# First routing stage: at most two of GpSimd's indexed scatters under way

## What is computed

```python
scores = jax.nn.sigmoid(x @ gate_w.T)                       # 32 experts
_, topk_ids = jax.lax.top_k(scores + e_bias[None, :], 4)
topk_w = jnp.take_along_axis(scores, topk_ids, axis=1)
topk_w = topk_w / jnp.sum(topk_w, axis=1, keepdims=True)
combine = zeros((T, E)).at[arange(T)[:, None], topk_ids].add(topk_w)
a = silu(einsum('th,ehi->tei', x, w1)) * einsum('th,ehi->tei', x, w3) * combine[:, :, None]
out = einsum('tei,eih->th', a, w2)
```

## Time and profile before

| | us |
|---|---|
| runs of the kernel before | 1258.39, 1265.16, 1267.11 (median 1265.16) |
| the profiled execution | 1277.19 |
| its span, first to last instruction | 1275.4 |
| first scatter issued | 329.91 |
| last scatter issued | 538.32 |
| first load of a list issued | 555.88 |
| first TensorE instruction of the experts' stage | 559.33 |

### The profile page before, as it was taken

How to read it: one execution, slowest core, us unless ns; L and a number is a source line. 1 busy time by engine, 2 the same in 40 slices (tenths; PEclk the granted TensorE clock), 3 DMA queues, 4 the chain that set the end, 5 groups by cost and what they waited for, 6 DMA issues and landing times. The chain is left out here.

```text
span 1275.4 us, 27327 instructions
## 1 busy us (share of the span) xinstructions
PE 941.0 (74%) x10334; PEld 714.0 (56%) x10334; DVE 717.1 (56%) x1742; ACT 572.5 (45%) x960; POOL 613.5 (48%) x582
## 2 busy tenths in 40 slices
PE   1478778875576655449995139888898889995998
PEld 1356566654232222149995017777777777885565
DVE  3455555542567555625554256566676776654565
ACT  1156666664566455326664013333333333332554
POOL 1256767564567746614444772453544631111454
PEclk9997888785778777769998578899899998998999
DMA  5221111101746945677775610413224223000001
GB/s 143 68 71 61 51 53 53 53 2 55 266 180 232 293 162 194 239 214 201 202 202 166 252 42 20 155 54 121 86 89 155 82 89 114 22 2 1 10 26 34
DMA packets 112065, 144.04 MB, mean 113 GB/s; under 512 B 14325, under 2 KB 93090, under 8 KB 105794
## 3 DMA queue, kind: packets, MB, share of 16 engines
q1 hardware_dynamic: 73026, 110.68, 25.6%
q0 software_dynamic: 8192, 16.79, 4.3%
q10 hardware_dynamic: 30720, 14.82, 4.0%
HBM read 76.60 MB, written 65.40 MB: 111 GB/s over the span
## 5 line engine op out<-in xcount | busy, mean ns | idle before, releaser
L917 POOL DMA_INDIRECT fetched_a<-rows_y,chosen_row x128 | 122.6, 958 | 172.9 <-DVE att_a L810 120.9
L438 POOL TENSOR_TENSOR p_lo_a<-probs_a,p_hi_a 128x1024 f16<-128x1024 f32 x64 | 136.3, 2129 | 88.3 <-ACT p_hi_a L297 88.1
L1474 POOL DMA_INDIRECT rows_x<-rows_r,index_r x128 | 136.1, 1063 | 79.4 <-DVE index_r L1378 42.5
L617 PEld LDWEIGHTS psum<-v_x_a,probs_a 128*128 128x128 f32 x1024 | 127.9, 201 | 3.4 <-issue 0.3
L617 PE MATMUL psum<-v_x_a,probs_a 128*128 128x65 f32 x1024 | 128.8, 282 | 0.0
L1652 POOL TENSOR_TENSOR h_lo_t<-hidden_t,h_hi_t 96x512 f16<-96x512 f32 x48 | 55.4, 1154 | 94.2 <-ACT h_hi_t L1620 94.2
L354 DVE TENSOR_REDUCE negmax_a<-psum 128x8 f32<-128x1024 f32 x64 | 78.2, 1223 | 23.4 <-PE psum L168 23.0
L795 DVE TENSOR_REDUCE negmax_a<-psum 128x8 f32<-128x1024 f32 x64 | 78.2, 1222 | 20.1 <-PE psum L602 9.7
L296 ACT ACTIVATE probs_a<-psum 128x1024 f32<-128x1024 f32 x64 | 65.5, 1023 | 45.4 <-PE psum L152 45.4
L668 PE MATMUL psum<-wo,att_t_a 128*128 128x128 f32 x512 | 63.9, 278 | 8.2 <-ACT att_t_a L729 5.8
L1398 DVE TENSOR_TENSOR k_out_r<-psum,k_out_r 128x512 f16<-128x512 f32 x64 | 42.1, 686 | 48.7 <-issue 29.3
(11 more groups left out here) (336 smaller groups left out, 2989.3 us busy)
## 6 DMA issues: line engine op xcount, KB each, us to landing
values<-v_out_r SPq DMA_DIRECT2D x16, 1040.0 KB
v_x_a<-values SPq DMA_DIRECT2D x16, 1040.0 KB
keys<-k_out_r SPq DMA_DIRECT2D x16, 1024.0 KB
listed_t<-rows_x SPq DMA_DIRECT2D x96, 128.0 KB, 2.3
rows_y<-result_t ACTq DMA_DIRECT2D x48, 256.0 KB, 2.4
k_a_a<-keys SPq DMA_DIRECT2D x16, 512.0 KB
k_b_a<-keys SPq DMA_DIRECT2D x16, 512.0 KB
q_pad_a<-narrow_q SPq DMA_DIRECT2D x64, 64.0 KB
```

What stands on the lines that cost most here:

```text
L438: nc.gpsimd.tensor_tensor(p_lo[:, s % RING0, :], probs[:, s % NPR, :], p_hi[:, s % RING0, :], ALU.subtract).then_inc(s_plo, 1)
L617: last_ = nc.tensor.matmul(PV[:, part, i * (HD + 1):(i + 1) * (HD + 1)], probs[:, s % 3, lane(part, i)], v_x[:, par, b % GB, h, :], start= ...
L917: nc.gpsimd.indirect_dma_start(fetched[:, b % NF1, k, :], None, rows_y, bass.IndirectOffsetOnAxis(ap=chosen["row"][:, b, k:k + 1], axis=0) ...
L1474: nc.gpsimd.indirect_dma_start(rows_x, bass.IndirectOffsetOnAxis(ap=index[:, g * GB + t, k:k + 1], axis=0), rows[:, g % 2, t, :, :].rearra ...
```

## The change

Scatter n of the stage, counted over all groups, first waits until scatter n - 2 has landed. For that the semaphore is chosen by the parity of n instead of that of the group. The wait on ScalarE is rewritten for the new counting: both semaphores must show that all scatters of groups up to g - 2 have landed. The final wait on SP (`s_scatter[0]` and `s_scatter[1]` at 256 x 4 each) stays as it is, 64 scatters of 16 on each.

```diff
@@ upper_rows(g), ScalarE @@
                     act.wait_ge(s_xhat, g + 1)
                     if g >= 2:
-                        act.wait_ge(s_scatter[g % 2], 256 * (g // 2))
+                        for n in range(2):
+                            act.wait_ge(s_scatter[n], 8 * 16 * (g - 1))
                         act.wait_ge(s_turn, g - 1)
@@ GpSimd @@
                     for t in range(GB):
                         for k in range(K0):
+                            n = (g * GB + t) * K0 + k
+                            if n >= 2:
+                                pool.wait_ge(s_scatter[n % 2], 16 * (n // 2))
                             nc.gpsimd.indirect_dma_start(
                                 rows_x, bass.IndirectOffsetOnAxis(ap=index[:, g * GB + t, k:k + 1], axis=0),
-                                rows[:, g % 2, t, :, :].rearrange("p h d -> p (h d)"), None).then_inc(s_scatter[g % 2], 16)
+                                rows[:, g % 2, t, :, :].rearrange("p h d -> p (h d)"), None).then_inc(s_scatter[n % 2], 16)
```

## The result

| | before | after |
|---|---|---|
| runs, us | 1258.39 to 1276.07, 4 runs, median 1266.13 | 1291.20 to 1298.85, 4 runs, median 1294.51 |
| ratio, 95% interval | 1 | 1.0234 [1.0195, 1.0273] |
| profiled execution | 1277.19 | 1293.93 |
| span | 1275.4 | 1292.1 |
| first, last scatter issued | 329.91, 538.32 | 327.72, 566.66 |

A forecast was written before the change was run, and what follows sets the result against it. The routing stage was taken as a chain in which GpSimd mostly waits for indices; burst losses of 3.9 us per ordinary group hide in idle time, and group 3's 7.2 us lateness remains: +7, 1272 us, range 1261 to 1304.

The forecast's parts named there:

- the forecast: Whole kernel: landings in bursts cost +7 us, 1272 against the median; own range +2 to +12, chance 0.43.
- the rival that prices a burst like the gather: Scatters in bursts: landing takes 5.93 us as in the second attention's gather, +45, 1310; chance 0.38 including values down to forecast.
- Quiet is free: Scatters while DMA is quiet: start to release takes 2.16 us, 0.36 below the free 2.52, so no loss.
- A met wait costs nothing: GpSimd's 126 added waits: one already met adds nothing, 0.31 us behind the one before against 0.30 without.
- L in a burst of stores: Scatter's start to its successor-but-one's start while DMA is full: 3.66 us, a pace of 1.83, 0.57 more than now.
- two lags of group 1: Group 1's scatters beside the values stores: 1.8 and 1.1 us behind the quiet case, taken as 1.5.
- Steps 1 to 3: Groups 0 to 2: each loses 3.9 us, partly hidden by idle time; group 3 starts 4.3 us late, at 411.3.
- Step 4: Group 3, with late weight loads: last scatter starts near 439.5, lands at 443.2, 7.2 us after ScalarE wants it.
- What is late next: ScalarE's rows buffer for group 5: first thing but GpSimd to be late, near 443 instead of 435.94, 7.2 us.
- Steps 5 and 6: Group 4 ends near 465, in time; groups 5 and 6 lose 3.9 each against 3.63 and 4.60 idle, nothing more.
- Step 7: Group 7 and SP's list load: last start 553.7, landed 557.3, wanted at 563.1; hidden, 5.8 us over.
- The rival of freed bandwidth: Stores and padding get through sooner when scatters are spread out: faster, down to 1253; chance 0.06, 0.04 beyond 1%.

The follow-up runs named there:

- depth one: The changed kernel with one scatter under way instead of two; a single run, 1433.16 us, against a median of 1271.23 for the kernel before on that chip.
- depth four: The changed kernel with four scatters under way instead of two (four semaphores); ratio to the kernel before 0.9995.
- both open: The changed kernel with the reciprocal deviation issued after four scatters, two groups ahead, and three rows buffers together; ratio to the kernel before 1.0242.
- early deviations: The changed kernel with GpSimd's reciprocal deviation for group g+2 issued after the first four scatters of group g; ratio to the kernel before 1.0185.
- three buffers: The changed kernel with three rows buffers instead of two, so ScalarE waits for the group three before; ratio to the kernel before 1.0211.
- long runs: The changed kernel with the late load of `L0_ffn_w2` in contiguous runs of 16 KB instead of 512-byte pieces; ratio to the kernel before 1.0229.
- late loads in group 6: The changed kernel with the three late weight loads moved from behind group 3's stores to group 6's; a single run, 1294.03 us.
- all but group 3: The kernel before with the wait for the scatter two places ahead in all groups except group 3; ratio to the kernel before 1.0166, two runs.
- the kernel with the lists first: The kernel before with the first four pairs of list loads issued ahead of the eight weight loads; ratio to the kernel before 1.0011.

## Why the prediction was right or wrong

Slower was held less likely (0.39) than no change that can be measured (0.57), and it was slower, by 2.3%; 1294.5 us is inside the range of 1261 to 1304, but far above the 1272 named and outside the forecast's own 1267 to 1277. It fell between the forecast and the rival that prices a burst like the gather, and it is that rival that had stretched the range so far: the range holds, the sum does not. What was right is the kind of price, landings in bursts that are waited for.

**Quiet is free: right, by a hair.** Gaps stay at 0.30 us. The value was not: the prediction added 1.75 us to the last byte and 0.41 us to the release for 2.16; depth one shows 2.49, so from the last byte to a released GpSimd it is 2.49 - 1.75 = 0.74 us. SP behind the padding, from which the 0.41 came, was not the same path. The margin is 0.03 us, not 0.36. The Trainium skill, in "DMA: Bandwidth & Descriptors", section "Anatomy of one DMA", fits 2.0 us plus bytes over 436 GB/s, an estimate of 2.15 us for 64 KB; the measured 2.49 us (to the next start, not to the completion alone) is 0.34 longer, and the measurement decides.

**A met wait costs nothing: right.** 124 waits at depth four, ratio 0.9995.

**L in a burst of stores: 3.66, measured 4.09 at the median.** By the prediction's own line (7 us at 3.66, 45 at 5.93) 4.09 gives 14 us: this term alone passes its 1% mark. The two lags of group 1 were 1.8 and 1.1 us, and I took the middle.

**Steps 1 to 3: about right in size, wrong in place.** Each ordinary group was to lose 3.9 us over 20.45; groups 0, 1, 5 and 6 lost 6.8, 5.7, 3.4 and 6.5 over their own time before, and group 2 lost 1.5. Group 3 was to start at 411.3 and did at 411.98.

**Step 4: the term that failed most.** Group 3 was to take 28.2 us (411.3 to 439.5; the terms written there, 421 + 17.6 + 2.15, give 440.7) and took 38.8 (411.98 to 450.76). The prediction put one L on all bursts; beside the late weight loads it is up to 10.56 us. The rows for it were there: slice and window showed the DMA engines full for 24 us, but the L was taken from group 1, where only stores run. The gather's 5.93 was called a bound from above, and it was none: depth one shows 9.00 with one under way.

**What is late next: half right.** The rows buffer was named as the first thing late, 7.2 us for group 5. It was 18.5 us (454.43 for 435.94), and by another door: VectorE waited 15.15 us for the reciprocal deviation, which stands on GpSimd behind the held scatters. The prediction did not list what is queued behind the waiting instruction on its own engine. The runs with one door or both open show that this omission did not make the time: the next door is shut just as long, and with both open the stage ends no earlier.

**Steps 5 and 6: wrong.** Group 4 was to end at 465 and did at 480.14 (26.9 us for it, where the prediction counted 23), and the index of group 5 came at 473.59 while GpSimd was still in group 4. With that the idle time ahead of groups 5, 6 and 7, into which those steps put their 3.9 us, was not there. The index idle was to fall from 42.5 to 20 to 25; it fell to 14.3, all ahead of group 0. From then on every further us in a landing is a us in the stage.

**Step 7: it had the wrong gate.** The prediction let SP's weight issues run ahead of the last scatter, so that only the list load waited for it, with 5.8 us to spare. The last scatter lies at 566.66, 13 us behind the 553.7 predicted, and the weight issues did not run ahead: in the kernels in which GpSimd's last group is held (after, early deviations, three buffers, both, long runs, late loads in group 6, and depth one) the first weight load follows the last scatter's start by 3.14 to 3.19 us, however long the padding has been over (6.50 us in the kernel with all but group 3, where the rest stays open). So the eight issues, 5.3 us, lie behind the last scatter and not ahead of it. By the prediction's rule the list load would have gone when the last scatter had landed, at 566.66 + 3.66 = 570.3; it went at 575.17, 4.9 us later. The padding's first issue went at 542.16, 13.9 us later than before (528.25), but its 16 issues on SP took 11.15 us where before they took 19.52, so the padding was no cover either. At the times that it predicted, the rule would still have held (553.7 + 3.2 = 556.9, ahead of SP's 558.2), by 1.3 us. The rule stated as a test ("if the list load follows at once, the tail was not covered") missed this, since it looked at the list load and not at the weight issues ahead of it.

**Nothing faster.** The rival of freed bandwidth had its point: traffic in 421 to 445 us fell from 328 to 287 GB/s, and ScalarE's pauses without a releaser and TensorE's 7.29 us are absent in the profile of after. But what they give back lies ahead of GpSimd, where it is worth nothing.

The balance: predicted +7; the burst's L at its measured value +14 by the prediction's line; group 3's landings beside loads 10.6 us more (38.8 - 28.2), and 5 us of weight issues behind the last scatter. That comes to 30, beside 28.4 measured between medians. It is a bookkeeping, not a proof: the terms overlap, and the kernel with the lists first gave such 5 us back behind TensorE's start, so that the last term may be worth nothing. What is shown is the bound (open doors change nothing), the place of the long landings (they move with the loads) and a depth at which the price is zero (four; three was not tried).

## What to carry to other kernels

A limit on indexed DMAs under way costs nothing only if (depth x issue step) exceeds the landing time in the worst traffic of the stage, not on average: here 2 x 1.26 us holds when it is quiet, 4 x 1.26 holds for nearly all, and beside weight loads a landing took 9 us with one under way and 10 to 13 with two. Size it from a run with one under way, which shows each landing as a step. And before pricing a delay, add it up against the slack of its engine through the whole stage: once that is used up the engine itself is the bound, and neither an earlier input nor another buffer brings anything back. Look as well at where a stage of the program ends: work of other engines that stands behind that boundary may start only when the slowed engine is through.

## What was not expected of the hardware

- A 64 KB indexed scatter with none of its kind ahead of it took 6.1 to 9.0 us from start to release while 2.6 MB of weights were loaded by SP, against 2.49 us when quiet and mostly 3.2 to 5.1 us beside large stores (once 7.06 us). The Trainium skill, in "DMA: Bandwidth & Descriptors", section "Latency and other measured facts", gives DRAM access 2 us at high load; here the excess over quiet is up to 6.5 us.
- Long contiguous pieces in the largest of those loads did not shorten it (two under way: longest wait 8.39 us, 6.23 with short ones).
- ScalarE has pauses of 2 to 10 us without a releaser on its core. They come at different places in different kernels, and the DMA engines need not be full in them (10.30 us in the kernel with all but group 3, with a DMA share of 0.13); their cause is open.
- SP's and ScalarE's first instructions of the next stage started together, 3.14 to 3.19 us after the start of GpSimd's last scatter, in seven kernels, in one of them 51 us after their own last work.
